# Dequantisation of a fused attention and FFN kernel: the scales' gather moved behind the difference, and the odd units' zero points taken on VectorE

## The reference

```python
def _dequant(qw, qz, sc, g_idx):
    shifts = jnp.arange(8, dtype=jnp.uint32) * 4
    wq = qw[:, None, :] >> shifts[None, :, None] & NIB      # 8 rows per 32-bit word
    wq = wq.reshape(-1, qw.shape[1]).astype(jnp.float32)
    zq = qz[:, :, None] >> shifts[None, None, :] & NIB
    zq = zq.reshape(qz.shape[0], -1).astype(jnp.float32) + 1.0
    return sc[g_idx] * (wq - zq[g_idx])

w_gu = _dequant(qweight_gu, qzeros_gu, scales_gu, g_idx_gu)   # [512, 2752]
w_d = _dequant(qweight_down, qzeros_down, scales_down, g_idx_down)  # [1376, 512]
gate, up = (x @ w_gu)[..., :1376], (x @ w_gu)[..., 1376:]
out = (silu(gate) * up) @ w_d
```

## Time and profile before

| | us |
|---|---|
| median of 3 runs (lowest, highest) | 871.94 (868.27, 872.51) |
| the profiled execution | 870.51 |
| its span in the profile | 868.8 |
| TensorE busy | 792.7 (91%) |
| VectorE busy | 488.0 (56%) |
| ScalarE busy | 427.9 (49%) |
| GpSimd busy | 297.3 (34%) |

### The profile page before, as it was taken

The page is one execution under the profiler, slowest core; times in us unless marked ns, Lnnn a source line. Parts: engine busy times, 40 slices in busy tenths (PEclk is TensorE's granted clock), DMA queues, the critical chain, the costliest instruction groups (busy, mean ns, idle before and its releaser), DMA issues.

```text
span 868.8 us, 24146 instructions
## 1 busy us (share of the span) xinstructions
PE 792.7 (91%) x10116; PEld 565.1 (65%) x10119; DVE 488.0 (56%) x1000; ACT 427.9 (49%) x817; POOL 297.3 (34%) x297
## 2 busy tenths in 40 slices
PE   5455778899999999999999999999999999999898
PEld 5411324465788578857885787578767876786484
DVE  9978663543656465746564656466646654554321
ACT  1656665452655265526652665266526662565120
POOL 2155455232145214521453144304430543054020
PEclk9655665999999999999999999999999999999899
DMA  8943223000010101011001100120011000100000
GB/s 276 264 119 88 59 73 85 26 3 2 26 29 3 50 27 29 3 51 35 21 3 49 46 9 3 51 53 2 3 49 53 2 3 25 29 3 14 13 2 24
DMA packets 21512, 37.04 MB, mean 43 GB/s; under 512 B 4158, under 2 KB 8414, under 8 KB 21404
## 3 DMA queue, kind: packets, MB, share of 16 engines
q1 hardware_dynamic: 21404, 35.48, 14.1%
HBM read 26.47 MB, written 4.19 MB: 35 GB/s over the span
## 4 chain that ended last, share of the span: by engine, by line
PE 70%; DVE 14%; issue 7%; ACT 7%; POOL 1%; DVEq 0%; ACTq 0%; POOLq 0%
PE bank L556 17%; PE bank L571 13%; PE bank L527 10%; PE bank L537 9%; PE bank L697 4%; PE bank L714 3%; DVE nmf L1275 3%; PE bank L583 3%; PE bank L690 3%; ACT arena L918 3%; PE bank L504 2%; PE bank L671 2%; DVE stats L1212 1%; DVE arena L1207 1%; DVE small L1060 1%
## 5 line engine op out<-in xcount | busy, mean ns | idle before, releaser
L556 PE MATMUL bank<-arena,WGU 128*128 128x256 f16 (+1 forms) x2112 | 248.4, 275 | 1.4 <-DVE arena L762 1.4
L556 PEld LDWEIGHTS bank<-arena,WGU 128*128 128x128 f16 (+1 forms) x2112 | 206.9, 101 | 28.1 <-DVE arena L762 1.7
L1463 POOL TENSOR_TENSOR arena<-arena 128x512 f16<-128x512 f32 x128 | 147.0, 1177 | 207.2 <-ACT arena L925 207.2
L571 PE MATMUL bank<-WD,arena 128*128 128x512 f16 (+1 forms) x528 | 121.0, 379 | 0.0
L918 ACT ACTIVATE arena<-bank,small 128x512 f32<-128x512 f32 x128 | 89.2, 776 | 54.9 <-PE bank L697 54.9
L1453 POOL TENSOR_TENSOR arena<-arena 128x512 f16<-128x512 f32 (+1 forms) x48 | 51.8, 1078 | 172.2 <-ACT arena L901 172.2
L527 PE MATMUL bank<-arena,WT 128*128 128x256 f16 x768 | 90.9, 281 | 2.9 <-DVE arena L762 2.5
L527 PEld LDWEIGHTS bank<-arena,WT 128*128 128x128 f16 x768 | 77.1, 101 | 16.3 <-issue 4.2
L537 PE MATMUL bank<-WT,arena 128*128 128x512 f16 x384 | 86.8, 383 | 0.0
L571 PEld LDWEIGHTS bank<-WD,arena 128*128 128x128 f16 (+1 forms) x528 | 49.3, 97 | 53.3
L1275 DVE TENSOR_REDUCE nmf<-bank 128x8 f32<-128x512 f32 x128 | 79.3, 681 | 5.6 <-PE bank L671 5.4
(11 more groups left out here) (172 smaller groups left out, 1002.2 us busy)
## 6 DMA issues: line engine op xcount, KB each, us to landing
arena<-in_L_ffn_qweight_gu SPq DMA_DIRECT2D x8, 688.0 KB, 5.5
arena<-arena SPq DMA_DIRECT2D x32, 144.0 KB, 2.7
WT<-in_ctx SPq DMA_DIRECT2D x8, 512.0 KB, 9.7
arena<-in_ctx SPq DMA_DIRECT2D x8, 512.0 KB, 3.7
arena<-in_x SPq DMA_DIRECT2D x8, 512.0 KB, 3.9
out_y<-arena SPq DMA_DIRECT2D x16, 256.0 KB, 2.0
arena<-in_L_ffn_qweight_down SPq DMA_DIRECT2D x10, 256.0 KB, 3.5
arena<-in_L_xattn_Wk SPq DMA_DIRECT2D x1, 1024.0 KB, 5.8
```

Of the source, the lines that this page charges most:

```text
L556: mm = e.matmul(pb[0:m, i * TOK:(i + 1) * TOK], WGU[:, sp, kb, half * INTER + fb * P:half * INTER + fb * P + m], x2T[:, mp, kb, :], start= ...
L571: mm = e.matmul(pb[:, :], hT[0:m, sp, fb, t * P:(t + 1) * P], WD[0:m, mp, fb, :], start=(n == 0), stop=(n == 3 * FB - 1))
L1463: e.tensor_tensor(phl[:, a, 1, :], pring[:, a, :], phl[:, a, 0, :], ALU.subtract).then_inc(S["p_lo"], 1)
```

## The change

On TensorE the scales' gather is issued last and alone waits for `d_w`; the zero points' gather comes first and waits only until the difference of unit n-2 has been read. An odd unit has no conversion and no identity matmul: VectorE adds `wint` and the gathered zero points straight into `dq` (`dve_dequant_sub`, in tick n+2, ahead of that tick's step 1), and the power of two moves into the product (L1207 becomes a scalar_tensor_tensor for odd units). Step 4 on ScalarE is left for even units alone. Even units keep their conversion on GpSimd. One semaphore `d_conv` stands for two; `d_zeros`, `d_sub` and `d_scale` are new.

```diff
 def pe_dequant(e, n):
+    reached(e, S["d_sub" if on_vector(n) else "d_scaled"], n // 2)
+    if on_vector(n):                                   # on_vector = lambda n: n % 2 == 1
+        e.matmul(diff[0:m, 0:cols], hot[0:groups, pick], z[0:groups, c0:c0 + cols],
+                 start=True, stop=True).then_inc(S["d_zeros"], 1)
+    else:
+        e.matmul(diff[0:m, 0:cols], hot[0:groups, pick], z[0:groups, c0:c0 + cols], start=True, stop=False)
+        e.wait_ge(S["d_conv"], n // 2 + 1)
+        e.matmul(diff[0:m, 0:cols], ident16[0:m, 0:m], wbf[n % 2][0:m, 0:cols], start=False, stop=True).then_inc(S["d_gathered"], 1)
     reached(e, S["d_w"], n - 1)
-    e.matmul(scale[0:m, 0:cols], hot[0:64 + groups, pick], sc3[0:64 + groups, c0:c0 + cols], start=True, stop=True)
-    e.matmul(diff[0:m, 0:cols], hot[0:groups, pick], z[0:groups, c0:c0 + cols], start=True, stop=False)
-    e.wait_ge(S[f"d_conv{n % 2}"], n // 2 + 1)
-    e.matmul(diff[0:m, 0:cols], ident16[0:m, 0:m], wbf[n % 2][0:m, 0:cols], start=False, stop=True).then_inc(S["d_gathered"], 1)
+    e.matmul(scale[0:m, 0:cols], hot[0:64 + groups, pick], sc3[0:64 + groups, c0:c0 + cols],
+             start=True, stop=True).then_inc(S["d_scale"], 1)

 def act_ticks(e, place):
     for n in ticks(place):
-        if n % 2:
-            dequant_conv(lambda out, src: e.activation(out, src, ACT.Copy), e, n)
         act_dequant_scaled(e, n - 2)                   # now returns at once for odd units
         act_dequant_hi(e, n - 4)

 def dve_ticks(e, place):
     for n in ticks(place):
+        dve_dequant_sub(e, n - 2)
         dve_dequant_int(e, n)                          # now waits for d_sub of unit n-2 (odd n)
         dve_dequant_w(e, n - 3)

+def dve_dequant_sub(e, n):                             # odd n only
+    e.wait_ge(S["d_int"], n + 1)
+    e.wait_ge(S["d_zeros"], n // 2 + 1)
+    reached(e, S["d_lo"], n - 3)
+    e.scalar_tensor_tensor(dq[n % 4][0:m, 0:cols], wint[n % 2][0:m, 0:cols], 1.0,
+                           dq_banks(n)[0][0:m, 0:cols], ALU.mult, ALU.add).then_inc(S["d_sub"], 1)

 def dve_dequant_w(e, n):
-    e.wait_ge(S["d_scaled"], n + 1)
+    if on_vector(n):
+        e.wait_ge(S["d_sub"], n // 2 + 1)
+        e.wait_ge(S["d_scale"], n + 1)
+        e.scalar_tensor_tensor(w, w, SCQ[0:m, 1:2] if down else SCQ[0:m, 0:1],
+                               dq_banks(n)[1][0:m, 0:cols], ALU.mult, ALU.mult).then_inc(S["d_w"], 1)
+        return
+    e.wait_ge(S["d_scaled"], n // 2 + 1)
+    e.wait_ge(S["d_scale"], n + 1)
     e.tensor_tensor(w, w, dq_banks(n)[1][0:m, 0:cols], ALU.mult).then_inc(S["d_w"], 1)
```

More of the change, by code:

```diff
@@ L274, in build @@
             "sc_high", "sc_rest", "hot_ready", "hotd_ready", "zd_ready",
-            "d_int", "d_conv0", "d_conv1", "d_gathered", "d_scaled", "d_w", "d_hi", "d_lo",
+            "d_int", "d_conv", "d_zeros", "d_sub", "d_gathered", "d_scale", "d_scaled", "d_w", "d_hi", "d_lo",
             "x_loaded", "ctx_loaded", "v_stacked", "y_stored0", "y_stored1",
@@ L463, in pe_ticks @@
                 pe_dequant(e, n - 2)
+        on_vector = lambda n: n % 2 == 1
         def dq_banks(n):
@@ L845, in act_dequant_scaled @@
         def act_dequant_scaled(e, n):
-            if not 0 <= n < ND:
+            if not 0 <= n < ND or on_vector(n):
                 return
@@ L852, in act_dequant_scaled @@
                 e.wait_ge(S["scq_ready"], 1)
-            e.wait_ge(S["d_gathered"], n + 1)
+            e.wait_ge(S["d_gathered"], n // 2 + 1)
             reached(e, S["d_lo"], n - 3)
@@ L864, in dequant_conv @@
             e.wait_ge(S["d_int"], n + 1)
-            reached(e, S["d_gathered"], n - 1)
-            copy(wbf[n % 2][0:m, 0:cols], wint[n % 2][0:m, 0:cols]).then_inc(S[f"d_conv{n % 2}"], 1)
+            reached(e, S["d_gathered"], n // 2)
+            copy(wbf[n % 2][0:m, 0:cols], wint[n % 2][0:m, 0:cols]).then_inc(S["d_conv"], 1)
         def act_qk(e, c, i, w, G):
@@ L1193, in dve_dequant_int @@
                 e.wait_ge(S[f"qw_loaded{i % 2}"], 16 * earlier)
-            reached(e, S[f"d_conv{n % 2}"], n // 2)
+            reached(e, S["d_sub" if on_vector(n) else "d_conv"], n // 2)
             at_col = (blk % 2) * DM if down else c0 % INTER
@@ L1198, in dve_dequant_int @@
                             ALU.logical_shift_right, ALU.bitwise_and).then_inc(S["d_int"], 1)
+        def dve_dequant_sub(e, n):
+            if not 0 <= n < ND or not on_vector(n):
+                return
+            _, (blk, down, c0, cols) = DQ_UNITS[n]
+            m = width(blk) if down else P
+            e.wait_ge(S["d_int"], n + 1)
[3 more added lines that the diff above has]
+                                   dq_banks(n)[0][0:m, 0:cols], ALU.mult, ALU.add).then_inc(S["d_sub"], 1)
         def dve_dequant_w(e, n):
@@ L1420, in pool_ticks @@
             for n in ticks(place):
-                if n % 2 == 0:
+                if not on_vector(n):
                     dequant_conv(e.tensor_copy, e, n)
```

## The result

The median went from 869.88 to 872.77 us (13 runs each, side by side); the ratio is 1.0037, 95% interval 1.0020 to 1.0054. So the changed kernel is slower by 1.7 to 4.7 us, and 874.8 had been forecast, +2.9 on the old median. The direction, the size and the named wait are those of the forecast. That the sum came out so close is partly luck: one place was mis-sized by nearly 3 us.

What follows compares the result with a forecast made beforehand. The gather-to-product loop, 3.76 us a pair, was taken to bound dequantisation, then a 4.2 us wait for GpSimd's low half. Places: 0.4 + 2.5 + 0.5 - 0.6 + 0.1 = +2.9 us, 874.8 at the median; range 866.5 to 879.

Steps and rivals of the forecast that it cites:

- What bounds the kernel: Dequantisation: a loop through gathers, identity matmul, ScalarE and product sets 3.76 us a pair; shortening it alone would gain.
- The wait that takes its place: VectorE's sum of an odd unit waits for GpSimd's low half of unit n-4: 4.2 us a pair against 3.76; chance 0.55.
- The price of the sum: VectorE's 17 added sums take 0.69 us each, as L1255; the odd product takes 0.75 for 0.69.
- Rival D: GpSimd's low half holds VectorE's sum like the shift: period 5.1, +8 on the main forecast, 882 us; chance 0.08.
- w0: Dequantisation ticks 6 to 11, 9.08 us long before: forecast +2.5 us.
- w1: Dequantisation ticks 12 to 19, up to the start of the key projection: forecast +0.5 us.
- keys: Dequantisation ticks 20 to 29: forecast -0.6 us, with ScalarE free earlier but GpSimd's two additions holding the masking.
- values: Dequantisation ticks 30 to 39: forecast +0.1 us, the drain at the end giving back what the loop took.
- Scales: Dequantisation ticks 0 to 5: forecast +0.4 us, with shift 5 held by the low half of unit 0 until 54.35.
- L1165 near 70 and the key projection near 91: Signs that the forecast is right: start times expected in the trace after the change.
- B: Loads bind, not the wait: VectorE's 2.6 plus two held shifts, about 3.3 us a pair; 866.5 us at the median; chance 0.22.
- C: TensorE's granted clock may rise later in the projections behind: up to 0.9 us each on key and query; 876.5 us; chance 0.15.

Runs made afterwards that it cites:

- e4: The kernel before with the scales' gather issued last, all units keeping conversion and identity matmul; ratio 0.9877 to the kernel before, -10.7 us.
- e5: The changed kernel with the scales' gather and its wait put back ahead of the zero points' gather; ratio 1.0179 to the kernel before, +15.6 us.
- e1: The changed kernel with five dq buffers for four; ratio 0.9971 to the kernel before, -2.5 us.
- e3: The changed kernel with GpSimd's low half ahead of its conversion; ratio 0.9931 to the kernel before, -6.0 us.
- e2: The changed kernel with GpSimd's memset moved from behind "scales" to behind "w1"; ratio 1.0012 to the kernel before, +1.0 us.
- second profiles: The kernel before and the changed kernel, each profiled again without edit; single runs of 871.15 and 875.52 us.
- e6: The changed kernel with five dq buffers and the memset behind "w1"; ratio 0.9929 to the kernel before, -6.2 us.
- e7: The changed kernel with GpSimd's low half ahead of its conversion and the memset behind "w1"; ratio 0.9940 to the kernel before, -5.2 us.

## Why the prediction was right

**What bounds the kernel.** Right, and too weak. The ring of scale gather, zero gather, identity matmul, ScalarE and product was the limit, and the forecast said that cutting it alone would be a gain. It did not price that gain. e4 does: 10.7 us. The change as a whole is that gain and a loss of 13.9 us by the odd units (from e4 to the changed kernel, 1.0037 less 0.9877). These two large terms, not a small one, make the +3.2. How they split depends on the order in which they are taken: the odd units alone, on the old gather order, cost 15.6 (e5).

**The wait that takes its place.** Right in each link and nearly to the tenth: the sum starts 1.93 us behind the end of its even shift (135.76 to 137.69; 1.83 forecast), idle 1.27 for 1.2, period 4.17 for 4.2. 15 waits were seen, 14 or 15 forecast. The odd shift, too, meets the low half as forecast: that one ends at 138.66, the shift 0.28 behind it (0.29 in the earlier trace rows), at 3.18 for 3.22. It is only 0.53 long, as it starts 0.25 ahead of the low half's end. The second low half by itself:

```profile
137.50 1.16 POOL L1458 TENSOR_TENSOR WD<-arena,WD 128x512 f16<-128x512 f32 x1
```

That it is this wait is shown twice, by another buffer (e1) and by another order (e3).

**The price of the sum.** 0.689 us with its uint32 input, as taken from L1255; the odd product 0.74 (0.75). Rival D is out: the sums never took more than 0.69, though they ran beside a low half (that at 137.69 beside the one at 137.50). By the rule of the Trainium skill that the prediction cites ("SBUF — State Buffer", "Who interferes with whom") they should not contend, with one input from SBUF, and the trace agrees.

**Place by place.** "w0", "w1", "keys" and "values" came within 0.15 us of the forecast each. In "keys" ScalarE began its activation (L881 before, now L887) 17.5 us behind shift 20, as forecast, not 18.6; and the masking was held by GpSimd's two additions, as said (L1257 took 2.36 us for two, 1.41), and ended at 22.7 for 22.8. "Scales" failed: +3.2 for +0.4. The step was "shift 5 is held by the low half of unit 0 until 54.35". It stood behind the memset that follows that low half as well, 2.0 us more (2.45 long, 0.49 in e2), a term that the forecast's sum does not have. e2 moved the memset, and the place, counted from GpSimd's first conversion, is 10.55 us long for 9.96 in the kernel before: +0.6, near the forecast +0.4. Of the rest of the miss, 0.8 us, 0.7 is that first conversion, which starts 2.88 behind shift 0 for 2.20 before. In the second profiles it was 3.05 and 2.58, over all kernels 0.55 to 3.05; nothing here ties it to the change. A smaller error helped: the one-hot table came 0.5 us faster, because its first instruction no longer meets a low half (0.87 for 1.40). The starts forecast from the beginning of the span, L1165 near 70 and the key projection near 91, were missed by 4 to 5 us (74.9 and 95.3): 1.9 by a longer set-up in that execution, 2.8 by "scales".

**The sum of it.** The places add to +5.6 in the first pair of profiles and +4.4 in the second, up to the start of the query projection, against +2.9 forecast and +1.7 to +4.7 measured over 13 runs. In the first pair 2.5 us come back by the value projection of chunk 1 (216.44 less 151.40 = 65.0, before 211.43 less 143.87 = 67.6), in the second none (67.7 and 67.5). What comes back is the clock, 0.9 in the query projection and 1.6 in the slow patch, and it varies from one execution to the next. The last FFN is 1.4 shorter in the first pair, the set-up 1.9 longer: with these the places give the spans' difference, 3.6; in the second pair, with 0.2 less of set-up, it is 4.4. How much comes back was read in these two pairs alone; whether it gives the changed kernel some 1.5 us on average, as the medians suggest, stays open. Without the memset's hold (e2) the kernel stands at +1.0. So the forecast's own terms, exact as they look, would have been about 2 us too high, and the missed one made up for that: that part of the agreement is luck.

**The rivals.** B named the right load, 3.3 us a pair, but for another kernel: it is what e6 shows once the wait is gone, with a "w0" of 10.6 us, though, where B had 8.0. C, the clock, is neither shown nor excluded: its sign, a key projection over 7.6 us, was there in the first profile of the changed kernel and not in the second (7.88 and 6.69; 7.18 and 7.11 in the kernel before).

## What to carry to other kernels

A buffer's free signal can be harmless on an engine that reads it late and costly on one that reads it early: when a step moves to another engine, ask where in that engine's order the wait now stands, and whether what it waits for is itself triggered by the instruction just ahead. Here a pair got 0.4 us longer although TensorE and ScalarE had less to do and GpSimd the same; exchanging two lines on GpSimd undid it. And a change of two parts is to be run as two: the first part alone beat every kernel that has the second by 4 us or more, and the second took back more than the first gave.

## What the runs showed of the hardware

- A nibble shift of VectorE (0.40 to 0.49 us alone) was held for the whole of a GpSimd memset that reads nothing: 2.45, 2.45 and 2.44 us (shift 5 in the changed kernel, e1 and e3), 2.35 and 2.60 (shift 19 in e2 and e7). L1126, with two SBUF inputs, had run beside the same memset in the kernel before: 3.19 us, 0.84 over the others of its line, with the 2.02 of the memset (from 54.61) inside it.
- A shift that already waits does not always get the next turn. Behind the low half that ended at 57.12 the memset went first (57.06), though the shift had stood there since 56.83. Between two low halves it was otherwise, in e6: the shift at 131.24 ended at 131.99, 0.28 behind the first, and the second took 1.34 us for 1.16. GpSimd's times are rough.

```profile
130.55 1.16 POOL L1458 TENSOR_TENSOR WD<-arena,WD 128x512 f16<-128x512 f32 x1
131.66 1.34 POOL L1458 TENSOR_TENSOR WD<-arena,WD 128x512 f16<-128x512 f32 x1
```

- A scalar_tensor_tensor with uint32 in SBUF and float32 in PSUM costs what the float32 form does, 0.689 us for 512 columns.
- Executions of one kernel differ by the clock. The same 264 matmuls of the last FFN took 31.82, 31.85 and 31.91 us in three profiles and 30.45 in the first of the changed kernel (granted clock 0.64 and 0.88 from 826 to 832 us in the two of the changed kernel), and its query projection 7.16 and 8.20 us, beginning at 1.2 GHz and ending at 2.4 in both. Two profiles of each kernel were needed to tell this from the change.
